# The closing sum over four expert outputs per token: half of the token tiles as products with diagonal weights

## What is computed

```python
probs = softmax(h @ router_w.T)
top_vals, top_idx = top_k(probs, 4)
top_vals = top_vals / top_vals.sum(-1)
y_e = (silu(h @ w_gate[e]) * (h @ w_up[e])) @ w_down[e]
routed = sum over k of top_vals[:, k] * y_e of expert top_idx[:, k]
shared = silu(h @ sh_gate) * (h @ sh_up) @ sh_down
x = x + routed + sigmoid(h @ sh_gate_w) * shared
```

## Time and profile before

| | us |
|---|---|
| median of 3 runs | 434.62 |
| lowest and highest of the 3 | 433.7, 436.66 |
| the profiled execution's own time | 436.41 |
| its span | 434.6 |

### The profile page before, as it was taken

How to read it: one execution, slowest core, us unless ns; L and a number is a source line. 1 busy time by engine, 2 the same in 40 slices (tenths; PEclk the granted TensorE clock), 3 DMA queues, 4 the chain that set the end, 5 groups by cost and what they waited for, 6 DMA issues and landing times.

```text
span 434.6 us, 6450 instructions
## 1 busy us (share of the span) xinstructions
PE 391.7 (90%) x1884; PEld 318.3 (73%) x1885; DVE 233.6 (54%) x514; ACT 149.2 (34%) x346; POOL 170.8 (39%) x159
## 2 busy tenths in 40 slices
PE   1999999999899999999999999969999999999600
PEld 1877888888688888888868778848888888888400
DVE  6865545545772112211254888737555555555467
ACT  2444343343443343424347343324323232323000
POOL 3501232132304444243311212362777777777500
PEclk9989999999999999999999999979999999999955
DMA  7401533435433332221111137550333333333284
GB/s 232 173 3 50 168 88 115 134 89 156 154 126 121 122 121 89 64 90 36 36 39 36 37 124 166 116 148 29 97 100 101 106 105 97 106 96 112 84 320 164
DMA packets 17214, 47.30 MB, mean 109 GB/s; under 512 B 3475, under 2 KB 5811, under 8 KB 16979
## 3 DMA queue, kind: packets, MB, share of 16 engines
q1 hardware_dynamic: 12682, 34.73, 25.8%
q0 software_dynamic: 4512, 12.33, 9.7%
HBM read 38.75 MB, written 8.29 MB: 108 GB/s over the span
## 4 chain that ended last, share of the span: by engine, by line
PE 80%; DVE 12%; DMA 3%; ACT 2%; issue 2%; POOL 0%; SPq 0%; POOLq 0%; DVEq 0%; ACTq 0%
PE gu L1033 12%; PE gu L1034 12%; PE gu L1035 12%; PE y L1303 9%; PE gu L1286 7%; PE y L1033 5%; PE y L1034 4%; PE y L1035 4%; DVE act_f L1023 3%; PE gu L1243 3%; PE gu L1295 2%; PE gu L1283 2%; PE gu L1288 2%; PE gu L1284 2%; PE gu L1059 2%
## 5 line engine op out<-in xcount | busy, mean ns | idle before, releaser
L455 POOL TENSOR_TENSOR w_lo<-w_raw,w_hi 128x512 fp32r<-128x512 f32 (+3 forms) x50 | 59.6, 1212 | 173.8 <-ACT w_hi L516 164.3
L1033 PE MATMUL gu<-act_hi,w_hi 128*128 128x512 f32 x196 | 78.4, 400 | 1.5 <-DVE hid L750 1.5
L1034 PE MATMUL gu<-act_lo,w_hi 128*128 128x512 f32 x196 | 77.2, 394 | 0.0
L1035 PE MATMUL gu<-act_hi,w_lo 128*128 128x512 f32 x196 | 76.8, 392 | 0.0
L540 ACT ACTIVATE hid_hi<-hid 128x512 fp32r<-128x512 f32 (+1 forms) x50 | 31.5, 633 | 93.5 <-DVE hid L750 53.2
L750 DVE TENSOR_TENSOR hid<-silu,gu 128x512 f32<-128x512 f32 (+1 forms) x28 | 19.2, 687 | 68.7 <-PE gu L1035 62.9
L490 POOL DMA_INDIRECT y_k<-w_raw,put x47 | 46.4, 986 | 23.4 <-issue 11.9
L763 DVE TENSOR_TENSOR hid_lo<-hid,hid_hi 128x512 fp32r<-128x512 f32 (+1 forms) x50 | 35.4, 711 | 30.2 <-ACT hid_hi L540 30.1
L1303 PE MATMUL y<-w_dn,t_hidT 88*128 x188 | 48.8, 383 | 0.6 <-DVE t_hidT L996 0.6
L1033 PEld LDWEIGHTS gu<-act_hi,w_hi 128*128 128x128 f32 x196 | 37.2, 190 | 10.7 <-issue 2.7
L532 ACT ACTIVATE silu<-gu 128x512 f32<-128x512 f32 (+1 forms) x50 | 29.7, 595 | 41.3 <-PE gu L1035 41.3
(11 more groups left out here) (183 smaller groups left out, 661.7 us busy)
## 6 DMA issues: line engine op xcount, KB each, us to landing
w_raw<-in_wc SPq DMA_DIRECT2D x8, 576.0 KB, 3.9
w_raw<-in_w SPq DMA_DIRECT2D x11, 384.0 KB, 3.2
w_raw<-in_w_gu SPq DMA_DIRECT2D x8, 352.0 KB, 4.3
w_gu<-in_w_gu SPq DMA_DIRECT2D x8, 352.0 KB, 4.7
w_gu<-y_k SPq DMA_DIRECT2D x5, 512.0 KB, 6.3
w_raw<-in_ws SPq DMA_DIRECT2D x6, 384.0 KB, 3.1
w_dn<-in_w_dn SPq DMA_DIRECT2D x1, 2288.0 KB
w_raw<-scr SPq DMA_DIRECT2D x8, 256.0 KB, 4.4
```

The lines of the kernel that those rows point to most:

```text
L455: nc.gpsimd.tensor_tensor(w_lo[par][:, w], w_raw[par][:, w], w_hi[par][:, w].bitcast(F32), ALU.subtract).then_inc(split, 1)
L1033: T.matmul(out, w[0], x[0], start=start, stop=False)
L1034: T.matmul(out, w[0], x[1], start=False, stop=False)
L1035: return T.matmul(out, w[1], x[0], start=False, stop=stop)
```

## The change

`SUM_ORDER` is 0, 4, 1, 5, 2, 6, 3, 7: loads, sums and outputs go in this order. For tiles 0 to 3 nothing else changes. For tiles 4 to 7 ScalarE, after its last silu, writes 16 blocks of 128x128: the identity (`cst`) scaled per partition by the weight of choice k, which is a matrix with the weights on its diagonal. They lie in `xT`. TensorE, after its last expert tile, multiplies for each of the four tiles the four diagonals with the four blocks of `y_in`, summing in one PSUM bank (Y[1][0], Y[1][1], GU[1][0], GU[1][1]). VectorE adds that bank to `base` in one instruction per tile.

```diff
+ON_PE = NT // 2
+SUM_ORDER = [t + h for t in range(ON_PE) for h in (0, ON_PE)]
...
+        s_diag, s_ysum = sem("weights_on_diagonals"), sem("choices_summed")
...
+        sum_ps = [Y[1][0], Y[1][1], GU[1][0], GU[1][1]]
+
+        def diag(t, k):
+            at = ((t - ON_PE) * K1 + k) * P
+            return xT[:, at // N, at % N:at % N + P]
...
-            for t in range(NT):
+            for t in SUM_ORDER:
                 sp.dma_start(y_in[t], d["y_k"][t * P * K1:(t + 1) * P * K1].rearrange("(p k) h -> p k h", k=K1)
                              ).then_inc(s_fin[t], 16)
-            for t in range(NT):
-                sp.wait_ge(s_fadd[t], K1)
+            for t in SUM_ORDER:
+                sp.wait_ge(s_fadd[t], K1 if t < ON_PE else 1)
                 sp.dma_start(d["out"][t * P:(t + 1) * P], base[:, t]).then_inc(s_out, 16)
...
             run_tiles(act, step)
+
+            for t in range(ON_PE, NT):
+                for k in range(K1):
+                    A.activation(diag(t, k), cst[:, CS_ID:CS_ID + P], ACT.Copy, scale=r_top[:, t, k:k + 1]).then_inc(s_diag, 1)
...
             dve.wait_ge(s_bc, 2 * KH)
-            for t in range(NT):
+            for t in SUM_ORDER:
+                if t >= ON_PE:
+                    dve.wait_ge(s_ysum, t - ON_PE + 1)
+                    V.tensor_tensor(base[:, t], base[:, t], sum_ps[t - ON_PE][:, 0:H], ALU.add).then_inc(s_fadd[t], 1)
+                    continue
                 dve.wait_ge(s_fin[t], 16)
...
             tile_down(last, last % 2, e[1])
+
+            for t in range(ON_PE, NT):
+                pe.wait_ge(s_diag, (t - ON_PE + 1) * K1)
+                pe.wait_ge(s_fin[t], 16)
+                for k in range(K1):
+                    ins = T.matmul(sum_ps[t - ON_PE][:, 0:H], diag(t, k), y_in[t][:, k], start=k == 0, stop=k == K1 - 1)
+                ins.then_inc(s_ysum, 1)
```

## The result

| | before | changed |
|---|---|---|
| median of 20 runs each, us | 436.88 | 434.24 |
| ratio of the changed kernel to before, 95% interval | | 0.9942 [0.9921, 0.9963] |
| profiled execution, its span | 434.6 | 430.5 |
| end of TensorE's last expert product | 409.61 | 408.16 |
| end of VectorE's last sum | 432.45 | 428.13 |

The change is worth 2.5 us (1.6 to 3.5) of 436.88, which is clear of noise; the forecast was -2.2. The time itself was forecast as 432.4 and came out at 434.24: the forecast started from the median of three runs, 434.62, and the kernel before has 436.88 over twenty. The two profiled spans differ by 4.1 us, but 1.45 of that lies ahead of TensorE's last expert product, where nothing was changed.

A forecast was written before the change was run, and what follows sets the result against it. VectorE's 32 gapless multiply-adds after TensorE's last product bound the end, loads close under. VectorE ends 2.3 us earlier, 0.1 allowed for output, sum -2.2: 432.4 us against the median 434.62, range 430.5 to 435.3.

The forecast's parts named there:

- What bounds it: After TensorE's last product: VectorE's 32 multiply-adds without a gap, 416.69 to 432.45, with the loads close under them.
- The clock, from two cases of the trace: TensorE's diagonal products start at 0.50 clock at 418.1; full clock returns between 421.5 and 425.0, taken as 424.
- the case of 6.9: Earlier in the trace: after 3.55 us idle, work resumed at 287.25 and the clock was full again at 294.14.
- The first rival: TensorE's four bursts: clock stays low, each takes 3.4 us, kernel slower by 0.4, 435.0; 12%.
- TensorE's prices: Each diagonal tile, eight records: 1.74 us at full clock, 2.0 from rest; 3.4 at half clock, 3.7 from rest.
- The additions: VectorE's four additions of a 128x256 PSUM block: 0.42 us each, 1.7 us together (1.4 to 2.7).
- The schedule: VectorE's order of waits after TensorE's last product: 9.6 us work, 3.9 idle for 15.8; ends at 430.15, 2.3 earlier.
- tile 7, hidden behind tile 3: End of the sums: TensorE done with tile 7 at 429.3, before VectorE ends tile 3 at 429.7.
- The outputs: Last two outputs issued 0.45 us apart instead of 1.97, 0.38 us each; 0.1 us allowed.
- ScalarE: 16 diagonals after its last work at 406.06: 4.3 us, at most 6.4, hidden with 5.5 us to spare.
- The signs: Forecast wrong if VectorE waits long before tile 7, loads last beyond 428, or the tile loop before 409 changes length.
- The second and third rivals: Second: clock back at 421.5, 432.0, 15%. Third: late loads land up to 1.5 us sooner, with early clock 431.0, 10%.

The follow-up runs named there:

- half loads: Changed kernel, changed kernel with 34 idle products, and kernel before, each loading only choices 0 and 1, used twice: tails 20.09, 17.67 and 23.18 us.
- the change once more: The changed kernel, unaltered, run and profiled again on another chip: tail 20.71 us, 0.9957 of before.
- the clock kept up: Changed kernel with 34 idle products of 512 columns between TensorE's last expert product and first diagonal one: tail 19.56 us, 0.9923 of before.
- the last load cut and the clock kept: Changed kernel with tile 4's addition behind tile 1's sums, tile 7's load cut in two, 34 idle products: tail 19.09 us, 0.9983 of before.

## Why the prediction was right

*What bounds it.* VectorE's 32 sums without a gap: right, shown by half loads leaving the tail of the kernel before alone.

*The clock, from two cases of the trace.* Right that it comes back during the second tile: 421.9 in the changed kernel. The delay was 4.9 us where 5.9 was taken. The same start in the other traces gave 3.1 (the change once more), 3.9, 4.6, 5.2 and 5.6: mostly inside the 3.4 to 6.9 read beforehand, once below it. In the case of 6.9 the clock was not low when the work resumed at 287.25; its mean over 287 to 288 is 0.65, so it fell at 287.3, and 6.9 is right as the time from the start of the work to the return. Which delay an execution gets was not predicted, and that this one lay near the middle is luck. The Trainium skill ("TensorE: Matmul & The Clock Gate", "HAM oscillation — how this bites in real kernels") describes bursts of about 2 us, each behind a DMA wait of about 3 to 5 us, that start at the lower clock every time. The waits between bursts are shorter here, and the clock did not fall in any: not in the pause of 0.48 us before the last tile, nor in pauses near 1.0 us with the clock kept up, nor in those of 1.00 and 1.41 us in the change once more. A wait of the skill's length is in the trace of the kernel before, 3.55 us until 287.25, and there the clock did fall, as the skill says. The first rival (clock low to the end) did not come about in any run.

*TensorE's prices.* 3.7 us from rest at the lower level, measured 3.75; 2.0 at the full one, measured 1.97.

*The additions.* The term was mis-sized: 0.45 us a step, 0.42 of it busy time. Busy time was right (0.41 to 0.42), but the next instruction starts 0.32 to 0.34 after the start: it does not wait for the sum, as the multiply-adds do for each other through s_fadd. Three steps shorter by 0.1 and the last one of 0.41 make 0.4 us.

*The schedule.* The tail was forecast at 20.5 (430.15 - 409.61) and measured at 19.97. The first sum starts 0.4 later behind the last expert product (7.5 for 7.1 us), the first stall is 3.1 for 3.2, the second stall of 0.7 us is not there because the clock came sooner, the additions give 0.4, and the four groups of multiply-adds take 0.2 more together. So the mechanism held, and the size came out close because errors of up to 0.7 us partly cancelled. The step "tile 7, hidden behind tile 3" is right in this profile, by 0.4 us: TensorE is done at 427.36, and VectorE comes to it at 427.72. In the change once more it failed, with the last load later and 1.00 us of waiting.

*The outputs.* 0.1 us allowed, 0.2 measured behind the last sum.

*ScalarE.* 4.3 us forecast, 4.78 measured, hidden by 7.5 us.

*The signs.* Of the signs of being wrong one did show: the tile loop ended 1.45 us sooner than in the kernel before. It is taken for scatter, since the six profiles taken where the kernel before takes some 437 us end it between 408.2 and 410.8, the two without the change at 409.6 and 410.8 and the four with it at 408.2, 408.6, 408.8 and 410.8. So the two spans, 434.6 and 430.5, show the gain of the change too large.

*The second and third rivals.* The clock was back early in the change once more, 3.1 us after the start, but the loads landed late there, and the tail was longer and not shorter. In the first profile the loads did land earlier, 13.3 us behind the first issue for 14.0, but that is not a property of the change: in the second profile of the same kernel it was 14.5. And its reason, fewer outputs among the loads, is not borne out: in the kernel before, with no output among them, the last load landed as late as ever.

## What to carry to other kernels

Work moved from the last busy engine to an idle one counts only as far as the two run side by side: order the pieces so that each engine's inputs arrive in turn, and find the next limit (here the loads, 0.4 us below in one profile and reached in another) before estimating. TensorE, idle for 8.8 us before its first tile here, took 3.75 us for it and 1.97 for its last: price the first piece at the lower clock and look at who is queued behind it. When two limits lie close together, single experiments show little for either; test them in a pair, with both removed, and profile the same kernel twice to know what scatter the small differences stand against.

The version with the clock kept up had the lowest ratio with whole loads, 0.9923 [0.989, 0.9957], but its interval overlaps the change's own; the shortest tail with whole loads, 19.09, belongs to the one with the last load cut and the clock kept, whose time ratio is not better. No version is shown to beat the change.

## What had not been expected of the hardware

On the second and third chip the kernel before takes 8 and 9% longer than on the first, and the changed kernel 8% on the second. In the changed kernel's trace there TensorE is busy 81.9 of the 100 us from 300 to 400, against 100.0 for the kernel before and the changed one in their first profiles; of its waits 7.0 us are for the turned hidden block and 6.3 us for the turned input tile. The granted clock has a mean of 0.97 in that stretch, against 1.00. All of that lies in the gather stage, ahead of what is studied here, and its cause is open.

Half the bytes bring the first loads in hardly sooner: in the three kernels with half loads (changed, changed with the clock kept up, before) the second landed 5.0, 4.6 and 4.3 us behind the first issue, and 4.6 to 5.0 in those with whole ones. What else sets it was not tried.
